# Expansion by source in halves of eight tiles, with 448-byte rows and a ScalarE copy

## The chip, the cores and the metric

The kernel runs on one core of a Trainium2 chip. The metric is the time of one execution in microseconds (us). A profile of one execution shows the engines PE (TensorE; PEld is its weight load), DVE (VectorE), ACT (ScalarE), POOL (GpSimd) and SP (SyncE, which here issues DMAs), and the DMA queues.

## The reference

Four graph layers run in a row on 12500 nodes of 64 features and 212500 edges, each layer behind a layer norm and a residual sum. The change touches the two middle ones:

```
# second layer: graph convolution
h   = features * deg_out ** -0.5 @ weight
rst = segment_sum(h[src], dst) * deg_in ** -0.5 + bias
# third layer: messages with edge features
msg = relu(x[src] + edge_attr)
agg = segment_sum(msg, dst)
h   = relu((x + agg) @ W1 + b1) @ W2 + b2
```

What matters here is `h[src]` and `x[src]`: one row of 64 numbers for every edge, read from the node table by the edge's source.

## The kernel before

The edges are sorted by source and padded to 1760 tiles of 128. `split_parts` writes the node table in SBUF as three bfloat16 parts (`m.parts`: high, middle and low, `PARTS` = 192 columns), whose sum is the fp32 value. `expand_by_source` (L1459) then makes one row per edge by a matmul with a one-hot matrix, writes the rows to DRAM, and `sum_by_target` (second layer) or `sum_messages_by_target` (third) fetches them in the order of the targets and sums them. The words "stage two" and "stage three" below mean the runs of `expand_by_source` for layer 2 and layer 3.

A stage works through 110 chunks of 16 tiles (`SB` = 16, 2048 edges); ten chunks are one body of a loop. No scheduler orders the work: each engine has its own hand-written list, and semaphores join them.

- **SP** (`step`, L1512): for chunk n it waits until the one-hot matrix of n is made, loads the lanes of chunk n+5 (L1496, 2048 bf16 numbers to all 128 partitions, 512 KB), in stage three also the edge features of chunk n+5 (L1500, 512 KB), and then stores the rows of chunk n (L1510) when they are ready.
- **DVE**: `turn` (L1555) makes the one-hot matrix of the next chunk from the lanes. In stage two `reach` (L1563, six instructions) prepares six small matmuls that locate groups, `put` (L1576) copies half of the results from PSUM to the rows as bf16, and `take` (L1568) reads the located groups. In stage three `add` (L1586, L1588, L1590) sums three parts and the edge features.
- **PE** (L1621 to L1651): for each quarter `u` of a chunk (four tiles, two PSUM banks) four matmuls of 192 columns (L1639). The columns' place in `m.parts` comes from the sorted block numbers: `run_values` (L1628, helper L801) loads eight numbers from SBUF into registers, twice a chunk. In stage two the odd quarters are followed by three small matmuls (L1647).
- **ACT**: in stage two it copies the even quarters (L1669); in stage three it applies Relu (L1666).
- **POOL**: in stage two it writes the target number of each edge into the last word of its row (L1686).

A row of stage two is 98 words (`ROW2`), 392 bytes: 192 bf16 parts, a one, and the target. `sum_by_target` gathers four rows (1568 bytes) per partition with an indirect DMA of POOL (L1936), reads the target number on DVE (L1832), and sums on PE. Beside that it splits edge features, which SP loads (L1767) and DVE prepares (L1805 to L1814).

Of the kernel before, what the change touches and what calls it, by code (L numbers as in the profile page):

```python
# [49 lines left out]
ROW2 = PARTS // 2 + 2  # L50
# [74 lines left out]
def allocate(nc, ctx):  # L125
# [41 lines left out]
    at += SB * P  # L167
    m.row_out = arena[:, at:at + 5 * SB * ROW2].rearrange("p (c t f) -> p c t f", c=5, f=ROW2)
# [16 lines left out]
    attr_onehot = arena[:, at:at + CB * P // 2]  # L185
    assert at + CB * P // 2 <= ARENA
# [40 lines left out]
    m.onehot_attr = [part.bitcast(BF16).rearrange("p (f s) -> p f s", s=CB) for part in (attr_onehot, tables[:, free:free + CB * P // 2])]  # L227
# [1231 lines left out]
def expand_by_source(nc, m, layer):  # L1459
# [9 lines left out]
    with ExitStack() as ctx:  # L1469
        s = sems(nc, "blank", "turned", "expanded", "put_act", "put_dve", "dst", "summed", "added", "row", "reached", "found", "taken", "zeros")  # L1470
# [14 lines left out]
        def sum_of(u, n):  # L1485

            return quad[:, 2 * u:2 * u + 2, 0:2 * PARTS].rearrange("p k (t f) -> p k t f", f=PARTS)[:, :, :, n * D:(n + 1) * D]

        def rows_of(ring_, c, u):

            return ring_[:, c % 5, 4 * u:4 * u + 4, :].rearrange("p (k t) f -> p k t f", t=2)

        @block.sync
        def _(sp):
            def lanes(n, c):
                sp.dma_start(m.lane_rows[:, c % 5, :], m.lanes_dram[bass.ds(n * (SB * P), SB * P)].partition_broadcast(P)  # L1496
                             ).then_inc(lanes_in[c % 5], 16)

            def attr(n, c):
                sp.dma_start(m.attr_rows[:, c % 5, :, :], records[:, bass.ds(n * SB, SB), REC_ATTR:REC]).then_inc(attr_in[c % 5], 16)  # L1500

            def store(n, c):
                if layer == 2:
                    sp.wait_ge(s["put_act"], n * 2 + 2 + 2)
                    sp.wait_ge(s["put_dve"], n * 2 + 2 + 2)
                    sp.wait_ge(s["dst"], n + 1)
                else:
                    sp.wait_ge(s["row"], n * 4 + 4)
                settle(sp)
                sp.dma_start(to_dram[bass.ds(n * (SB * P), SB * P), :].rearrange("(t p) f -> p t f", p=P), out[:, c % 5, :, :]  # L1510
                             ).then_inc(stored[c % 5], 16)

            def step(n, c, more):
                if more:
                    sp.wait_ge(s["turned"], n + 1)
                    settle(sp)
                    lanes(n + 5, c)
                if more == "all":
                    if layer == 3:
                        sp.wait_ge(s["added"], n * 4 + 4 + 4)  # L1520
# [12 lines left out]
            for c in range(chunks):  # L1533
                step((BODIES - 1) * chunks + c, c, "all" if c < chunks - 5 else "lanes" if c == chunks - 5 else "")
            for c in range(5):
                sp.wait_ge(stored[c], 16 * (TS // SB // 5))
            sp.wait_ge(s["zeros"], 16)

        @block.vector
        def _(dve):  # L1540
            v = nc.vector
            if layer == 2:
                v.memset(out16[:, :, :, PARTS:PARTS + 2].rearrange("p c t f -> p (c t) f"), 1.0).then_inc(s["blank"], 1)
                dve.wait_ge(s["blank"], 1)
            v.sem_inc(s["expanded"], 2 * 4)
            v.sem_inc(s["put_dve"], 2)
            v.sem_inc(s["taken"], 2)
            v.sem_inc(s["added"], 4)

            def turn(i, c):  # L1550
                n = i * chunks + c
                dve.wait_ge(lanes_in[c % 5], i * (chunks // 5 * 16) + c // 5 * 16 + 16)

                dve.wait_ge(s["expanded"], n * 4 + 4)
                v.tensor_scalar(m.turned16[:, c % 2, :], m.lane_rows[:, c % 5, :], m.lane_no[:, :], None, ALU.is_equal  # L1555
                                ).then_inc(s["turned"], 1)

            def reach(i, c):
                n = i * chunks + c

                dve.wait_ge(s["expanded"], n * 4 + 4)
# [4 lines left out]
            def take(i, c, u):  # L1566
                n = i * chunks + c
                v.tensor_reduce(m.found[:, bass.ds(n * SET + u // 2 * (SET // 2), SET // 2)],  # L1568
                                quad[:, 2 * u + 1, FOUND:FOUND + 3 * (SET // 2)].rearrange("p (e n) -> p e n", n=3), AX, ALU.add
                                ).then_inc(s["taken"], 1)  # L1570

            def put(i, c, u):
                n = i * chunks + c
                dve.wait_ge(s["expanded"], n * 4 + u + 1 + 2 * 4)
                to = rows_of(out16, c, u)[:, :, :, 0:PARTS]
                v.tensor_copy(to, quad[:, 2 * u:2 * u + 2, 0:2 * PARTS].rearrange("p k (t f) -> p k t f", f=PARTS)).then_inc(s["put_dve"], 1)  # L1576
                take(i, c, u)

            def add(i, c, u):
                n = i * chunks + c  # L1580
                k = n * 4 + u
                dve.wait_ge(s["expanded"], k + 1 + 2 * 4)
                if u == 0:
                    dve.wait_ge(attr_in[c % 5], i * (chunks // 5 * 16) + c // 5 * 16 + 16)
                to, attr = rows_of(out, c, u), rows_of(m.attr_rows, c, u)
                v.tensor_tensor(to, sum_of(u, 0), attr, ALU.add).then_inc(s["summed"], 1)  # L1586
                dve.wait_ge(s["summed"], 2 * k + 1)
                v.tensor_tensor(to, to, sum_of(u, 1), ALU.add).then_inc(s["summed"], 1)  # L1588
                dve.wait_ge(s["summed"], 2 * k + 2)
                v.tensor_tensor(to, to, sum_of(u, 2), ALU.add).then_inc(s["added"], 1)  # L1590

            def body(i, first):
                for c in range(chunks):
# [6 lines left out]
                    if not first or c >= 5:  # L1600
# [18 lines left out]
        def _(pe):  # L1619
            parts = m.parts.rearrange("p b f -> p (b f)")  # L1620
            with pe.Fori(0, BODIES) as i:  # L1621
                for c in range(chunks):
                    n = i * chunks + c
                    pe.wait_ge(s["turned"], n + 1)
                    for u in range(4):
                        k = n * 4 + u
                        if u % 2 == 0:
                            numbers = run_values(nc, ENG.PE, m.sorted_block[:, bass.ds(n * SB + 4 * u, 8)], NB)  # L1628

                        if layer == 3:  # L1630
                            pe.wait_ge(s["added"], k + 1)
                        elif u % 2:
                            pe.wait_ge(s["put_dve"], n * 2 + u // 2 + 1)
                            pe.wait_ge(s["taken"], n * 2 + u // 2 + 1)
                        else:
                            pe.wait_ge(s["put_act"], n * 2 + u // 2 + 1)
                        settle(pe)
                        for j in range(4):
                            done = nc.tensor.matmul(quad[:, 2 * u + j // 2, j % 2 * PARTS:(j % 2 + 1) * PARTS],  # L1639
                                                    m.turned16[:, c % 2, (4 * u + j) * P:(4 * u + j + 1) * P],  # L1640
                                                    parts[:, bass.ds(numbers[4 * (u % 2) + j] * PARTS, PARTS)], start=True, stop=True)
                        if layer == 2 and u % 2:
                            for e in range(SET // 2):
                                g = u // 2 * (SET // 2) + e
                                if e == 0:
                                    pe.wait_ge(s["reached"], n * SET + g + SET // 2)
                                done = nc.tensor.matmul(quad[:, 2 * u + 1, FOUND + 3 * e:FOUND + 3 * e + 3],  # L1647
# [6 lines left out]
        def _(act):  # L1654
            a = nc.scalar

            def body(i, first):
                for c in range(chunks):
# [3 lines left out]
                    for u in range(4):  # L1662
                        if layer == 3:
                            act.wait_ge(s["added"], n * 4 + u + 1 + 4)
                            rows = out[:, c % 5, 4 * u:4 * u + 4, :]
                            a.activation(rows, rows, ACT.Relu).then_inc(s["row"], 1)  # L1666
                        elif u % 2 == 0:
                            act.wait_ge(s["expanded"], n * 4 + u + 1 + 2 * 4)
                            a.activation(rows_of(out16, c, u)[:, :, :, 0:PARTS],  # L1669
                                         quad[:, 2 * u:2 * u + 2, 0:2 * PARTS].rearrange("p k (t f) -> p k t f", f=PARTS),  # L1670
                                         ACT.Copy).then_inc(s["put_act"], 1)

            act.sem_inc(s["put_act"], 2)
# [4 lines left out]
        if layer == 2:  # L1678
            @block.gpsimd
            def _(pool):  # L1680
                def body(i, first):
                    for c in range(chunks):
# [3 lines left out]
                        nc.gpsimd.tensor_copy(m.row_out[:, c % 5, :, ROW2 - 1:ROW2],  # L1686
# [10 lines left out]
def sum_by_target(nc, m, a, layer):  # L1697
# [9 lines left out]
    with ExitStack() as ctx:  # L1707
# [72 lines left out]
        def _(dve):  # L1780
# [39 lines left out]
            with dve.Fori(0, BODIES_D) as i:  # L1820
                if layer == 2:
                    add_bias(i * SHARE)
                for c in range(BODY_D):
# [7 lines left out]
                    if layer == 2:  # L1831
                        v.tensor_tensor(lanes.rearrange("p (g t) -> p g t", t=GRAN),  # L1832
                                        m.ring2[:, c % deep, :, ROW2 - 1].rearrange("p (g t) -> p g t", t=GRAN),
# [1083 lines left out]
```

## Time and profile before

| | us |
|---|---|
| three runs | 8924.55, 8933.99, 8934.04 (median 8933.99) |
| profiled execution | 8922.76 |
| its span, first to last instruction | 8920.1 |
| stage two, first instruction to the first gather after it | 3132.9 to 3900.8 |
| summing of layer 2, first to last gather | 3900.8 to 4814.7 |
| stage three, first to last store issued | 4913.6 to 5588.3 |

Over the whole span PE is busy 71%, DVE 66%, POOL 55% and ACT 28%, but these are means over stages with different limits; the two expansions are 1440 us of the span and are read by themselves. Times in rows are microseconds from the start of the span. A row of a timeline gives the start, the duration, the engine, the line, the operation, its tiles and shape, how many (x), and in brackets how long the engine was idle before and what ended that. "issue" there means that the profile shows no semaphore or DMA for which the engine waited. PEq or PEldq marks instructions of PE's sequencer.

### The profile page before, as it was taken

To read this page: it belongs to the slowest core of one execution; us is meant where nothing else is said; L and a number is where in the kernel's file an instruction comes from. 1 tells how busy PE (TensorE), PEld (TensorE's weight loads), DVE (VectorE), ACT (ScalarE), POOL (GpSimd) and SP (SyncE) were. 2 spreads that over 40 slices of the span, in tenths; PEclk is the share of its full clock that TensorE was granted. 3 is DMA by queue.
4 is the path that set the end of the run, shared out by engine and by line. 5 is a ranking of instruction groups with operands and counts; after the bars stand their busy time and mean duration, and the time that the engine had idled before them with its cause. 6 is when DMAs were issued, how large, how long until landed. Compare 5 with 4: busy or idle time off the path is not lost. (4 is left out here: it accounts for less than half of the span.)

```text
span 8920.1 us, 183726 instructions
## 1 busy us (share of the span) xinstructions
PE 6289.7 (71%) x35446; PEld 4927.1 (55%) x35447; DVE 5909.6 (66%) x18166; ACT 2529.7 (28%) x8033; POOL 4865.1 (55%) x4975
## 2 busy tenths in 40 slices
PE   2688888888847645556664555788668888888886
PEld 1577777777735433345553222566456666666664
DVE  8566666666669755568887888899554444444444
ACT  5355555555511222211110222111112221222222
POOL 0477777777756200047773000677347777777773
PEclk9555555555555655568886555999855555555556
DMA  6655555454546399987786999666633333333333
GB/s 133 152 154 149 156 148 154 149 156 147 156 97 139 72 190 195 195 198 224 230 226 130 246 257 257 181 181 178 92 111 82 80 80 80 81 81 80 82 80 30
DMA packets 1822628, 1295.50 MB, mean 145 GB/s; under 512 B 1262870, under 2 KB 1643574, under 8 KB 1820576
## 3 DMA queue, kind: packets, MB, share of 16 engines
q1 hardware_dynamic: 1580112, 841.10, 39.9%
q0 software_dynamic: 200704, 415.20, 17.9%
q10 hardware_dynamic: 40912, 29.67, 1.5%
q14 instruction: 638, 5.23, 0.2%
q8 instruction: 262, 4.29, 0.2%
HBM read 923.76 MB, written 361.78 MB: 144 GB/s over the span
## 5 line engine op out<-in xcount | busy, mean ns | idle before, releaser
L1138 POOL DMA_INDIRECT sorted_edges<-arena,idx x1664 | 1619.0, 973 | 727.8 <-issue 638.7
L2253 POOL DMA_INDIRECT arena<-node_table,idx x1760 | 1660.4, 943 | 557.0 <-issue 388.9
L1053 PE MATMUL banks<-arena,edge_tables 128*128 x3520 | 1164.7, 439 | 288.3 <-DVE edge_tables L982 233.8
L2229 PE MATMUL banks<-arena 128*128 128x64 f32 x3520 | 1214.1, 448 | 0.0
L1639 PE MATMUL banks<-arena 128*128 x3520 | 670.9, 361 | 769.2 <-issue 435.2
L1053 PEld LDWEIGHTS banks<-arena,edge_tables 128*128 128x128 f32 x3520 | 898.5, 317 | 417.6 <-issue 393.3
L2224 PE MATMUL banks<-arena 128*64 128x65 f32 x3520 | 843.0, 343 | 401.0 <-ACT arena L2240 400.3
L2128 POOL DMA_INDIRECT arena<-expanded,idx x576 | 544.6, 945 | 1003.5 <-DVE idx L2005 788.5
L2229 PEld LDWEIGHTS banks<-arena 128*128 128x128 f32 x3520 | 883.4, 311 | 210.2
L2240 ACT ACTIVATE arena<-arena 128x64 f32<-128x64 f32 x1760 | 450.1, 257 | 1787.2 <-DVE arena L2192 1781.6
L2199 DVE TENSOR_TENSOR arena<-arena,banks 128x64 f32 x1760 | 387.8, 220 | 820.2 <-PE banks L2229 792.8
L1639 PEld LDWEIGHTS banks<-arena 128*128 128x128 bf16 x3520 | 367.0, 104 | 1012.2 <-issue 931.8
L955 DVE SCALAR_TENSOR_TENSOR edge_tables<-iota_row,edge_tables,banks 128x99 f32<-128x99 f32 x1664 | 528.9, 318 | 594.2 <-PE banks L1035 582.4
L2224 PEld LDWEIGHTS banks<-arena 128*64 128x64 f32 x3520 | 509.5, 206 | 627.4 <-ACT arena L2240 451.9
L1936 POOL DMA_INDIRECT arena<-expanded,idx x576 | 659.3, 1145 | 274.9 <-issue 146.5
L1104 ACT ACTIVATE arena<-arena,edge_tables 128x64 f32<-128x64 f32 x1664 | 446.2, 337 | 912.8 <-DVE arena L992 903.4
L982 DVE TENSOR_SCALAR edge_tables<-arena,shift_row 128x128 f32 x1760 | 526.6, 299 | 171.4 <-issue 94.1
L1085 ACT ACTIVATE edge_tables<-base,edge_tables 128x99 bf16<-128x99 bf16 x1664 | 491.0, 368 | 201.3 <-issue 132.2
L1033 PE MATMUL banks<-per_node,from 128*128 128x99 bf16 x1664 | 467.0, 281 | 72.2 <-DVE per_node L945 70.6
L1063 PE MATMUL banks<-w_pair,arena 128*128 128x128 f32 x1664 | 485.8, 448 | 0.0
L1039 PE MATMUL banks<-edge_tables,per_node 128*99 128x99 bf16 x1664 | 451.0, 271 | 47.9 <-ACT edge_tables L1085 47.9
L2192 DVE TENSOR_TENSOR arena<-arena,banks 128x64 f32<-128x64 f32 x1760 | 375.9, 215 | 162.6 <-DMA arena<-node_table,idx 157.4
(426 smaller groups left out, 11712.5 us busy)
## 6 DMA issues: line engine op xcount, KB each, us to landing
arena<-sorted_edges SPq DMA_DIRECT2D x220, 524.0 KB
arena<-lanes_dram SPq DMA_DIRECT2D x222, 512.0 KB, 8.0
expanded<-arena SPq DMA_DIRECT2D x110, 784.0 KB, 8.0
arena<-in_attr_rows SPq DMA_DIRECT2D x576, 130.0 KB
arena<-sorted_edges SPq DMA_DIRECT2D x110, 536.0 KB
arena<-row_keys SPq DMA_DIRECT2D x110, 512.0 KB
arena<-sorted_edges SPq DMA_DIRECT2D x110, 512.0 KB, 5.6
expanded<-arena SPq DMA_DIRECT2D x110, 512.0 KB
```

The source lines that it names most:

```text
L955: v.scalar_tensor_tensor(m.junk[:, j % 2, 0:BUCKETS], m.iota_row[:, 0:BUCKETS], m.bucket[:, bass.ds(n, 1)], rank, ALU.is_equal, ALU.mult, ...
L982: v.tensor_scalar(m.onehot[:, j % 4, :], m.row_ring[:, bass.ds(slots[j] * P, P)], first_lane[:, j:j + 1], None, ALU.is_equal).then_inc(s[" ...
L1053: nc.tensor.matmul(m.psum[j % 4][:, 0:D], m.onehot[:, j % 4, :], m.support[:, bass.ds(blocks[j] * D, D)], start=True, stop=True).then_inc( ...
L1063: product = nc.tensor.matmul(m.psum[bank_of(n)][:, e * P:(e + 1) * P], m.pair_ring[c % 2][:, pair * P:(pair + 1) * P], m.w_pair[:, :], sta ...
L1085: a_.activation(m.below[:, (QUAD * n + e) % 8, 0:BUCKETS], m.base16[:, 0:BUCKETS], ACT.Sign, bias=m.pack[:, bass.ds(t, 1), 1], scale=-SHRU ...
L1138: nc.gpsimd.indirect_dma_start(m.sorted, bass.IndirectOffsetOnAxis(ap=m.idx[:, j % (4 * CH):j % (4 * CH) + 1], axis=0), m.out_ring[:, slot ...
L1639: done = nc.tensor.matmul(quad[:, 2 * u + j // 2, j % 2 * PARTS:(j % 2 + 1) * PARTS], m.turned16[:, c % 2, (4 * u + j) * P:(4 * u + j + 1) ...
L1936: nc.gpsimd.indirect_dma_start(to, None, rows, bass.IndirectOffsetOnAxis(ap=m.idx[:, c % aims * groups + g:c % aims * groups + g + 1], axis=0)
L2128: nc.gpsimd.indirect_dma_start(m.ring3[:, at:at + GRAN * row], None, rows, bass.IndirectOffsetOnAxis(ap=m.idx[:, c % aims * groups + g:c % ...
L2224: nc.tensor.matmul(m.psum[GRAM][0:D, 0:RW], row[:, 0:D], row, start=False, stop=False, skip_group_check=True)
L2229: nc.tensor.matmul(m.psum[j % 4][:, 0:D], m.onehot8[:, c % 4, j % CB, :], row[:, 0:D], start=True, stop=True).then_inc(s["summed"], 1)
L2253: nc.gpsimd.indirect_dma_start(slots[:, j % SLOTS, 0:D], None, m.table, bass.IndirectOffsetOnAxis(ap=m.idx[:, j % SLOTS:j % SLOTS + 1], ax ...
```

## The change

Both expansions are now written for halves `h` of eight tiles (four PSUM banks each) in place of quarters of four.

- PE loads the 16 block numbers of a chunk with one `run_values` at the top of the chunk, ahead of the wait for the one-hot matrix. It waits per half, not per quarter. In stage two both halves are followed by their three small matmuls, as the odd quarters were.
- In stage two ACT copies each whole half (1536 numbers per partition) in one instruction, after DVE's `take` of that half. DVE copies nothing. The semaphores `put_act` and `put_dve` become one, `put`.
- In stage three DVE's three sums and ACT's Relu run on 512 numbers per partition in place of 256, half as often.
- Rows of stage two are 112 words, 448 bytes. The target number keeps its place (word 97); words 98 to 111 are set to zero once, by a second memset, for which ACT waits before it first frees the PSUM halves. The store carries 896 KB per chunk (784 KB before), a gather 1792 bytes per partition (1568).
- One one-hot buffer of `sum_by_target` moves from the arena to the edge tables to make room.

```diff
-ROW2 = PARTS // 2 + 2
+ROW2 = 112
+COUNT2 = PARTS // 2
+DST2 = COUNT2 + 1
...
     def store(n, c):
         if layer == 2:
-            sp.wait_ge(s["put_act"], n * 2 + 2 + 2)
-            sp.wait_ge(s["put_dve"], n * 2 + 2 + 2)
+            sp.wait_ge(s["put"], n * 2 + 2 + 2)
             sp.wait_ge(s["dst"], n + 1)
         else:
-            sp.wait_ge(s["row"], n * 4 + 4)
+            sp.wait_ge(s["row"], n * 2 + 2)
...
 def body(i, first):   # DVE
     for c in range(chunks):
         turn(i, c + 1)
         if layer == 2:
             reach(i, c)
-        for u in range(4):
+        for h in range(2):
             if layer == 3:
-                add(i, c, u)
-            elif u % 2:
-                put(i, c, u)
+                add(i, c, h)
+            else:
+                take(i, c, h)
...
 # PE
+numbers = run_values(nc, ENG.PE, m.sorted_block[:, bass.ds(n * SB, SB)], NB)
 pe.wait_ge(s["turned"], n + 1)
-for u in range(4):
-    if u % 2 == 0:
-        numbers = run_values(nc, ENG.PE, m.sorted_block[:, bass.ds(n * SB + 4 * u, 8)], NB)
+for h in range(2):
...
 # ACT
-            elif u % 2 == 0:
-                act.wait_ge(s["expanded"], n * 4 + u + 1 + 2 * 4)
+            else:
+                act.wait_ge(s["expanded"], n * 2 + h + 1 + 2 * 2)
+                act.wait_ge(s["taken"], n * 2 + h + 1 + 2)
```

In the two listings below the names in brackets are semaphores as the built program calls them: lane_26 is `turned`, ended_27 `expanded`, rows_28 is `put_act` before and `put` after, variance_35 is `taken`; kept_39 and brought_40 belong to the loads of lanes. ISA rows set registers or wait.

On PE, between the two halves of a chunk of stage two, the order before is:

```order
L1647 MATMUL banks<-edge_tables,arena 128x3
L801 ISA
L801 TENSOR_LOAD target_plan
L1636 REGISTER_ALU
L1639 ISA [waits rows_28]
L1639 MATMUL banks<-arena 128x192
```

and after:

```order
L1638 MATMUL banks<-edge_tables,arena 128x3
L1625 REGISTER_ALU
L1630 ISA [waits rows_28,variance_35]
L1630 MATMUL banks<-arena 128x192
L1630 ISA
```

The register load is gone from this place; the other one, at the top of the chunk, stays and loads 16 numbers.

On DVE, one chunk of stage two before:

```order
L1555 TENSOR_SCALAR arena<-arena,lane_no 128x2048 [waits ended_27,brought_40]
L1563 TENSOR_SCALAR arena<-iota_row,edge_tables 99x128 [waits ended_27]
L1563 TENSOR_SCALAR arena<-iota_row,edge_tables 99x128 x5
L1576 CAST arena<-banks 128x4x192 [waits ended_27]
L1568 TENSOR_REDUCE edge_tables<-banks 128x3
```

and after:

```order
L1557 TENSOR_SCALAR arena<-arena,lane_no 128x2048 [waits ended_27,kept_39]
L1565 TENSOR_SCALAR arena<-iota_row,edge_tables 99x128 [waits ended_27]
L1565 TENSOR_SCALAR arena<-iota_row,edge_tables 99x128 x5
L1571 TENSOR_REDUCE edge_tables<-banks 128x3 [waits ended_27] x2
L1557 TENSOR_SCALAR arena<-arena,lane_no 128x2048 [waits ended_27,brought_40]
```

The pair of CAST and TENSOR_REDUCE stood twice in a chunk; both copies have left DVE, and the two reductions now wait for PE themselves.

## Rows read from the trace of the kernel before

**Rows 1.** Windows: length, busy PE, PEld, DVE, ACT, POOL, clock, DMA share, GB/s.

```profile
3500.00:3700.00 200.00, 106.22 (x645) 67.10 (x644) 114.57 (x324) 47.30 (x59) 7.77 (x30) 0.50 1.13 196
...
5200.00:5400.00 200.00, 104.12 (x526) 54.58 (x524) 177.69 (x424) 54.53 (x131) 0.00 (x0) 0.50 1.12 256
```

**Rows 2.** One tile (expanded rows): durations in ns min/median/max, first and last start.

```profile
L1936 POOL DMA_INDIRECT arena<-expanded,idx x576: 940/977/2739, 3900.8 to 4814.7; - x192
...
L1525 SPq DMA_DIRECT2D expanded<-zero x2: 332/336/339, 3132.9 to 4913.6; - x2
```

**Rows 3.** Timeline of one chunk of stage two.

```profile
3505.37 0.74 DVE L1555 TENSOR_SCALAR arena<-arena,lane_no 128x2048 bf16<-128x2048 bf16 x1
...
3505.40 1.46 PE L1639 MATMUL banks<-arena 128*128 x8 [1.01 <-issue]
3505.60 0.40 SPq L1510 DMA_DIRECT2D expanded<-arena  x1
...
3506.03 1.26 DVE L1563 TENSOR_SCALAR arena<-iota_row,edge_tables 99x128 bf16<-99x128 f32 x6
...
3506.25 0.81 ACT L1669 ACTIVATE arena<-banks 128x768 bf16<-128x768 f32 x1 [1.92 <-PE banks L1639]
...
3506.87 0.48 PE L1647 MATMUL banks<-edge_tables,arena 99*128 x3
...
3507.39 0.96 DVE L1576 CAST arena<-banks 128x768 bf16<-128x768 f32 x1
...
3509.48 1.46 PE L1639 MATMUL banks<-arena 128*128 x8 [2.13 <-issue]
...
3512.23 0.34 PE L1639 MATMUL banks<-arena 128*128 x1 [1.04 <-issue]
```

**Rows 4.** Register loads: two of stage two; four-number loads of 3950 to 4780.

```profile
L801 PEldq TENSOR_LOAD <-target_plan x1: 591/591/591, 3504.4 to 3504.4; - x1
...
L801 PEldq TENSOR_LOAD <-target_plan x1: 1786/1786/1786, 3507.3 to 3507.3; - x1
...
L801 PEldq TENSOR_LOAD <-target_plan x130: 330/334/622, 3952.6 to 4777.5; - x130
```

**Rows 5.** Waits of SP, 3200 to 3800: total us, times, longest.

```profile
SPq L796 <- DVE arena L1576: 316.6, 88, 4.3
```

**Rows 6.** ACT copies of 512 and 256 numbers just ahead of stage two.

```profile
L1440 ACT ACTIVATE arena<-banks x4: 395/583/598, 3127.1 to 3128.6; 128x512 bf16<-128x512 f32 x3, 128x256 bf16<-128x256 f32 x1
```

**Rows 7.** DMA: a store's issue, packets of 3880-3881.75, 3882-3883.5, then 5586-5591.5.

```profile
3879.04 0.38 SPq L1510 DMA_DIRECT2D expanded<-arena  x1
...
q1 hardware_dynamic: 1167, 0.46, 96.4%
...
q1 hardware_dynamic: 725, 0.28, 115.6%
...
q1 hardware_dynamic: 4631, 1.18, 95.9%
```

**Rows 8.** Stage three: SP's timeline, then DVE's wait and adds, 4960 to 5540.

```profile
5251.72 2.07 SPq L1496 DMA_DIRECT2D arena<-lanes_dram  x1
5254.14 0.39 SPq L1500 DMA_DIRECT2D arena<-sorted_edges  x1
5254.84 2.59 SPq L1510 DMA_DIRECT2D expanded<-arena  x1
5257.74 2.06 SPq L1496 DMA_DIRECT2D arena<-lanes_dram  x1
...
DVE arena L1555 <- DMA arena<-lanes_dram: 32.8, 78, 0.8
...
L1590 DVE TENSOR_TENSOR arena<-arena,banks 128x256 f32<-128x256 f32 x382 | 160.6, 420 | 13.1
```

**Rows 9.** Summing of layer 2: gather queue of 4000-4600, a wait of 3950-4780.

```profile
q0 software_dynamic: 24539, 76.95, 45.8%
...
DVE edge_tables L1805 <- DMA arena<-in_attr_rows: 104.3, 110, 4.7
```

More of the change, by code:

```diff
@@ L167, in allocate @@
     at += SB * P
+    assert ROW2 * 5 * SB <= 10 * SB * D and DST2 < ROW2
     m.row_out = arena[:, at:at + 5 * SB * ROW2].rearrange("p (c t f) -> p c t f", c=5, f=ROW2)
@@ L184, in allocate @@
     at += SB * P
-    attr_onehot = arena[:, at:at + CB * P // 2]
-    assert at + CB * P // 2 <= ARENA
+    assert at <= ARENA
     at = NB * PARTS
@@ L226, in allocate @@
     assert AIMED * 3 <= TD
-    m.onehot_attr = [part.bitcast(BF16).rearrange("p (f s) -> p f s", s=CB) for part in (attr_onehot, tables[:, free:free + CB * P // 2])]
+    m.onehot_attr = [part.bitcast(BF16).rearrange("p (f s) -> p f s", s=CB) for part in (tables[:, 4 * TP:4 * TP + CB * P // 2], tables[:, free:free + CB * P // 2])]
     m.attr_parts = [tables[:, TSX + n * PARTS:TSX + (n + 1) * PARTS] for n in range(2)]
@@ L1469, in expand_by_source @@
     with ExitStack() as ctx:
-        s = sems(nc, "blank", "turned", "expanded", "put_act", "put_dve", "dst", "summed", "added", "row", "reached", "found", "taken", "zeros")
+        s = sems(nc, "blank", "turned", "expanded", "put", "dst", "summed", "added", "row", "reached", "found", "taken", "zeros")
         lanes_in = ring(nc, "lanes_in", 5)
@@ L1483, in expand_by_source, with sum_of, half_of @@
         FOUND = 2 * PARTS
[L1485 to L1491, printed above, removed]
+        HALF = SB // 2
+        def sum_of(h, n):
+            return quad[:, 4 * h:4 * h + 4, 0:2 * PARTS].rearrange("p k (t f) -> p k t f", f=PARTS)[:, :, :, n * D:(n + 1) * D]
+        def half_of(ring_, c, h):
+            return ring_[:, c % 5, HALF * h:HALF * h + HALF, :].rearrange("p (k t) f -> p k t f", t=2)
         @block.sync
@@ L1519, in step @@
                     if layer == 3:
-                        sp.wait_ge(s["added"], n * 4 + 4 + 4)
+                        sp.wait_ge(s["added"], n * 2 + 2 + 2)
                         settle(sp)
@@ L1543, in _ @@
                 v.memset(out16[:, :, :, PARTS:PARTS + 2].rearrange("p c t f -> p (c t) f"), 1.0).then_inc(s["blank"], 1)
-                dve.wait_ge(s["blank"], 1)
-            v.sem_inc(s["expanded"], 2 * 4)
-            v.sem_inc(s["put_dve"], 2)
+                v.memset(out16[:, :, :, PARTS + 4:2 * ROW2].rearrange("p c t f -> p (c t) f"), 0.0).then_inc(s["blank"], 1)
+            v.sem_inc(s["expanded"], 2 * 2)
             v.sem_inc(s["taken"], 2)
-            v.sem_inc(s["added"], 4)
+            v.sem_inc(s["added"], 2)
             def turn(i, c):
@@ L1552, in turn @@
                 dve.wait_ge(lanes_in[c % 5], i * (chunks // 5 * 16) + c // 5 * 16 + 16)
-                dve.wait_ge(s["expanded"], n * 4 + 4)
+                dve.wait_ge(s["expanded"], n * 2 + 2)
                 v.tensor_scalar(m.turned16[:, c % 2, :], m.lane_rows[:, c % 5, :], m.lane_no[:, :], None, ALU.is_equal
@@ L1559, in reach @@
                 n = i * chunks + c
-                dve.wait_ge(s["expanded"], n * 4 + 4)
+                dve.wait_ge(s["expanded"], n * 2 + 2)
                 for e in range(SET):
@@ L1564, in reach, with take, add @@
                                     None, ALU.is_ge).then_inc(s["reached"], 1)
-            def take(i, c, u):
+            def take(i, c, h):
                 n = i * chunks + c
-                v.tensor_reduce(m.found[:, bass.ds(n * SET + u // 2 * (SET // 2), SET // 2)],
-                                quad[:, 2 * u + 1, FOUND:FOUND + 3 * (SET // 2)].rearrange("p (e n) -> p e n", n=3), AX, ALU.add
+                dve.wait_ge(s["expanded"], n * 2 + h + 1 + 2 * 2)
+                v.tensor_reduce(m.found[:, bass.ds(n * SET + h * (SET // 2), SET // 2)],
+                                quad[:, 4 * h + 3, FOUND:FOUND + 3 * (SET // 2)].rearrange("p (e n) -> p e n", n=3), AX, ALU.add
                                 ).then_inc(s["taken"], 1)
[L1572 to L1583, printed above, removed]
+            def add(i, c, h):
+                k = (i * chunks + c) * 2 + h
+                dve.wait_ge(s["expanded"], k + 1 + 2 * 2)
+                if h == 0:
                     dve.wait_ge(attr_in[c % 5], i * (chunks // 5 * 16) + c // 5 * 16 + 16)
-                to, attr = rows_of(out, c, u), rows_of(m.attr_rows, c, u)
-                v.tensor_tensor(to, sum_of(u, 0), attr, ALU.add).then_inc(s["summed"], 1)
+                to, attr = half_of(out, c, h), half_of(m.attr_rows, c, h)
+                v.tensor_tensor(to, sum_of(h, 0), attr, ALU.add).then_inc(s["summed"], 1)
                 dve.wait_ge(s["summed"], 2 * k + 1)
-                v.tensor_tensor(to, to, sum_of(u, 1), ALU.add).then_inc(s["summed"], 1)
+                v.tensor_tensor(to, to, sum_of(h, 1), ALU.add).then_inc(s["summed"], 1)
                 dve.wait_ge(s["summed"], 2 * k + 2)
-                v.tensor_tensor(to, to, sum_of(u, 2), ALU.add).then_inc(s["added"], 1)
+                v.tensor_tensor(to, to, sum_of(h, 2), ALU.add).then_inc(s["added"], 1)
             def body(i, first):
@@ L1599, in body @@
                         reach(i, c)
-                    if not first or c >= 5:
+                    if layer == 3 and (not first or c >= 5):
                         dve.wait_ge(stored[c % 5], i * (chunks // 5 * 16) + c // 5 * 16)
-                    for u in range(4):
+                    for h in range(2):
                         if layer == 3:
-                            add(i, c, u)
-                        elif u % 2:
-                            put(i, c, u)
+                            add(i, c, h)
+                        else:
+                            take(i, c, h)
             body(0, True)
@@ L1623, in _ @@
                     n = i * chunks + c
+                    numbers = run_values(nc, ENG.PE, m.sorted_block[:, bass.ds(n * SB, SB)], NB)
                     pe.wait_ge(s["turned"], n + 1)
-                    for u in range(4):
-                        k = n * 4 + u
-                        if u % 2 == 0:
-                            numbers = run_values(nc, ENG.PE, m.sorted_block[:, bass.ds(n * SB + 4 * u, 8)], NB)
+                    for h in range(2):
                         if layer == 3:
[L1631 to L1634, printed above, removed]
-                        else:
-                            pe.wait_ge(s["put_act"], n * 2 + u // 2 + 1)
+                            pe.wait_ge(s["added"], n * 2 + h + 1)
+                        else:
+                            pe.wait_ge(s["put"], n * 2 + h + 1)
+                            pe.wait_ge(s["taken"], n * 2 + h + 1)
@@ L1637, in _ @@
                         settle(pe)
[L1638 to L1642, printed above, removed]
+                        for j in range(HALF):
+                            t = HALF * h + j
+                            done = nc.tensor.matmul(quad[:, t // 2, t % 2 * PARTS:(t % 2 + 1) * PARTS],
+                                                    m.turned16[:, c % 2, t * P:(t + 1) * P],
+                                                    parts[:, bass.ds(numbers[t] * PARTS, PARTS)], start=True, stop=True)
@@ L1643, in _ @@
+                        if layer == 2:
                             for e in range(SET // 2):
-                                g = u // 2 * (SET // 2) + e
+                                g = h * (SET // 2) + e
                                 if e == 0:
                                     pe.wait_ge(s["reached"], n * SET + g + SET // 2)
-                                done = nc.tensor.matmul(quad[:, 2 * u + 1, FOUND + 3 * e:FOUND + 3 * e + 3],
+                                done = nc.tensor.matmul(quad[:, 4 * h + 3, FOUND + 3 * e:FOUND + 3 * e + 3],
@@ L1661, in body @@
                         act.wait_ge(stored[c % 5], i * (chunks // 5 * 16) + c // 5 * 16)
-                    for u in range(4):
+                    for h in range(2):
                         if layer == 3:
-                            act.wait_ge(s["added"], n * 4 + u + 1 + 4)
-                            rows = out[:, c % 5, 4 * u:4 * u + 4, :]
+                            act.wait_ge(s["added"], n * 2 + h + 1 + 2)
+                            rows = out[:, c % 5, HALF * h:HALF * h + HALF, :]
                             a.activation(rows, rows, ACT.Relu).then_inc(s["row"], 1)
-                        elif u % 2 == 0:
-                            act.wait_ge(s["expanded"], n * 4 + u + 1 + 2 * 4)
[L1669 to L1673, printed above, removed]
+                        else:
+                            act.wait_ge(s["expanded"], n * 2 + h + 1 + 2 * 2)
+                            act.wait_ge(s["taken"], n * 2 + h + 1 + 2)
+                            a.activation(half_of(out16, c, h)[:, :, :, 0:PARTS],
+                                         quad[:, 4 * h:4 * h + 4, 0:2 * PARTS].rearrange("p k (t f) -> p k t f", f=PARTS),
+                                         ACT.Copy).then_inc(s["put"], 1)
+            if layer == 2:
+                act.wait_ge(s["blank"], 2)
+                act.sem_inc(s["put"], 2)
             body(0, True)
@@ L1685, in body @@
                         settle(pool)
-                        nc.gpsimd.tensor_copy(m.row_out[:, c % 5, :, ROW2 - 1:ROW2],
+                        nc.gpsimd.tensor_copy(m.row_out[:, c % 5, :, DST2:DST2 + 1],
                                               m.dst_sorted[:, bass.ds((i * chunks + c) * SB, SB)].unsqueeze(2)).then_inc(s["dst"], 1)
@@ L1832, in _ @@
                         v.tensor_tensor(lanes.rearrange("p (g t) -> p g t", t=GRAN),
-                                        m.ring2[:, c % deep, :, ROW2 - 1].rearrange("p (g t) -> p g t", t=GRAN),
+                                        m.ring2[:, c % deep, :, DST2].rearrange("p (g t) -> p g t", t=GRAN),
                                         m.block_at[:, bass.ds(n * groups, groups)].unsqueeze(2).to_broadcast([P, groups, GRAN]),
```

## Prediction

> **What bounds the kernel now.** The change lies in two stages of 110 chunks and, by the longer rows, in the summing after the first of them, so I read the windows by stage first, then the timeline of one chunk, then the DMA queues.
>
> Stage two runs from 3132.9 to 3900.8, 768 us [rows 2]. DVE issues 11 instructions a chunk there (one turn, six for reach, two copies, two reductions), and 324 of them in 200 us [rows 1] are 29.45 chunks: 6.79 us a chunk. PE is busy 53% of that, DVE 57%, and the DMA share stands above 1 at 196 GB/s [rows 1]; so both PE and the queues could be the limit. The timeline decides. PE's first block starts at 3505.40, its small matmuls end at 3507.35, then PE is idle for 2.13 us "on issue"; the second block runs from 3509.48 to 3511.19 (the next start at 3512.23 less 1.04), and 1.04 us are idle again [rows 3]. That closes the period of 6.83: blocks of 1.95 and 1.71, gaps of 2.13 and 1.04. Both gaps hold a register load, of 1.786 and 0.591 us [rows 4]; the rest of each gap, 0.34 and 0.45, is waits and address arithmetic. Nothing else is late there: the copies of the bank halves end (3507.06 on ACT) well before PE comes back to them. SP waits for DVE 316.6 us in 600 [rows 5], so the stores wait for compute and not the other way round. Stage two is bound by PE's own list, half of whose idle time is one slow register load.
>
> Why that load takes three times as long as the other isn't in the rows; what they show is where it stands. It starts 1.7 us after a store was issued at 3505.60 [rows 3, 4], while the store's rows leave SBUF: the store issued at 3879.04 has 1892 of its 2048 packets between 3880 and 3883.5 [rows 7], so a store occupies the queues until about 4.5 us after its issue. The fast load comes 5.6 us after the previous store's issue, one period back.
>
> Stage three is another case. SP issues lanes, features and store one behind the other, 2.07, 0.39 and 2.59 us with 0.3 us between them, and begins again after 6.02 us [rows 8]: there is no room in its list for a wait on compute. DVE, 89% busy [rows 1], waits for lanes in 78 chunks of about 96 [rows 8], though these are ordered five chunks ahead. Stage three is bound by SP and the queue behind it, at 256 GB/s [rows 1].
>
> **The change part by part.** Stage two, on PE. One register load goes, the other loads 16 numbers. Four numbers take 0.334 us and eight 0.591 [rows 4], 64 ns each, so 16 come to 1.11 us (at least 0.59, if the load has a flat part; at most 2.3, if it is slowed as the slow one is). With 0.45 us of waits around it, two blocks of 1.71 (the 0.24 us that the first block lost to reach goes: DVE's turn and reach now begin behind a reduction, 0.16, and three of the six reach steps are done 1.5 us after the previous chunk, while PE needs them at 2.7) and 0.25 us between the halves, for which the bounds are 0 and 0.45, PE's period is 1.11 + 0.45 + 1.71 + 0.25 + 1.71 = 5.23 us.
>
> On ACT a copy of 1536 numbers replaces one of 768. 256 take 0.395, 512 about 0.59 [rows 6] and 768 take 0.81 [rows 3], so 1536 come to 1.47 us, two of them to 2.9 us a chunk. The copy of a half starts 0.25 us after PE is done (take is now ahead of it) and ends 1.7 us after; PE wants the same banks back after 1.11 + 0.45 + 1.71 + 0.25 = 3.5 us. So the new wait costs nothing with 1.8 us to spare; what is queued behind it on ACT is only the next copy, and the store on SP, which goes out about 0.9 us later than now, with five row buffers behind it. DVE loses two copies of 0.96 us [rows 3] a chunk, worth nothing, because DVE isn't the limit.
>
> Stage two, on the queues. A chunk moves 896 KB of rows and 512 KB of lanes, 1.442 MB. Rows of 256 bytes take 18.2 ns a packet and hold that for 5.5 us; rows of 392 bytes take 23.1 ns at first and 38.3 ns in the later part of the same store (share times 16 engines times the window, over the packets) [rows 7]. For 448 bytes the line through 256 and 392 gives 25 ns; with today's slow part it would be 33 to 42. The nearest row for the sum of rows and lanes is stage three, with 256-byte rows and the same lanes: at its 256 GB/s a chunk takes 5.63 us. At today's 196 GB/s it takes 7.36 us. I take the first, because 448 bytes, like 256 and unlike 392, is a whole number of 64-byte pieces and the slow part appears with 392 alone; that this is the reason is a guess.
>
> Against this stands the Trainium skill: "DMA: Bandwidth & Descriptors", section Specifications, says that transfers under 512 B make the DMA read, modify and write. By that rule 448 bytes would be as badly off as 392, and the sum would go by 196 GB/s. The 256-byte stores don't show such a loss.
>
> So the queues (5.63) and PE (5.23, and more when a store slows the load) lie close, and I take 5.65 us a chunk: (6.79 - 5.65) x 110 = 125 us gained. The ends: 5.23, or 172 us, and 7.36, or 63 us lost.
>
> Stage three: six of twelve DVE sums go. From 256 (0.42) [rows 8] to 768 numbers (0.96) [rows 3] DVE needs about 1.05 ns a number, so a sum of 512 takes 0.69 in place of 0.84 and DVE gains 0.9 us a chunk. SP's list is as long as before, so I book 0; what DVE gains it waits longer for lanes.
>
> Summing of layer 2: gathers grow by 14%. Their queue takes 45.8% of the 16 engines in 600 us [rows 9], so about 6.5% more, 59 us over 915 us if nothing hid it. DVE is the busiest engine there and waits 104.3 us of 830 for edge features behind those gathers [rows 9]; if that wait grows by a tenth, the loss is 12 us. Bounds 0 and 59; I take 12. The larger memset at the start hides behind the loading of the first lanes.
>
> Sum against the profiled execution: 8922.8 - 125 + 12 = 8810 us. The median of the runs is 11 us above that execution and the fastest run 2 us; I put the median at 8815.
>
> **The rivals.**
> - *The store slows the long load in every chunk.* The store is issued about 1.9 us after the last matmul of its chunk, and with a period of 5.2 the load starts 3.3 us behind it, within the 4.5 us. With the 1.2 us that the slow load loses now, the period is 6.43 and the gain 40 us: 8900. Against it: at 6.4 us the next load starts behind the store and is fast again.
> - *The rows stay slow, and the queues take over: slower.* If they move no more than 196 GB/s, the chunk takes 7.36 us, 63 us are lost and 12 more in the summing: 9000. It decides as soon as the rate stays below 1.442 MB in 6.79 us, 212 GB/s. For it speak the DMA share above 1 already now and the page's rule; against it the fast 256-byte rows and that SP waits for DVE now.
> - *The queues give way entirely.* Then PE's 5.23 stands: 8922.8 - 172 + 12, or 8768 for the median.
> - *Stage three gains too*, because SP's long issues follow DVE after all: 99 us more, 8716. Its SP rows speak against it.
> - *Little happens*, since the rate settles near 212 GB/s and one limit takes the place of the other: 8930.
>
> **How the numbers follow.** Forecast 8815: 0.47. Load slowed: 0.15. PE alone: 0.15. Slower: 0.10. Little: 0.07. Stage three too: 0.06. A measurement of this kernel tells 0.2%, 18 us, from no change. Faster by more than that: 0.47 + 0.15 + 0.15 + 0.06 = 0.83; within: 0.07; slower: 0.10. The range reaches from just under PE's case to just over the slowed load, 8750 to 8905, and leaves out stage three, the slower case and half of little.
>
> **What would show it.** In stage two: one register load a chunk on PE, of 1.1 us or up to 2.3 beside a store; a period of 5.2 to 5.8; ACT copies of 1.47 us; the queue at 250 GB/s or more and 448-byte packets near 25 ns. In stage three: SP without waits, the same 6.0 us, and DVE waiting longer for lanes. In the summing: the wait of L1805 somewhat over 104 us. I am wrong if the 448-byte rows are slower than 30 ns on the mean, if SP stops waiting for compute in stage two, or if the period of stage three moves.

## The result, and the profile after

The changed kernel takes 8782.95 us (median of 4 runs, 8779.7 to 8794.44) where the kernel before, on the same chip, takes 8932.7: a ratio of 0.9837, interval 0.9819 to 0.9854. The profiled execution of after is its slowest, 8794.44 us with a span of 8792.7; against the span before (8920.1), 127.4 us are gone. The medians lie 149.8 apart, because the profiled execution of before is faster than all its timed runs. Where the 127.4 went, read from the first and last starts of the rows of the expanded tile (columns as in [rows 2]):

```profile
L1930 POOL DMA_INDIRECT arena<-expanded,idx x576: 943/977/2746, 3738.7 to 4673.7; - x192
...
L1528 SPq DMA_DIRECT2D expanded<-zero x2: 332/338/343, 3135.4 to 4777.1; - x2
```

Stage two runs from 3135.4 to 3738.7, 603.3 us where it took 767.9 [rows 2]: -164.6. The summing of layer 2 follows, from the first gather to the last one ahead of stage three: 935.0 where the kernel before takes 913.9, +21.1. Stage three, from its store of zeros to the first gather of layer 3 (5460.0, before 5600.0), takes 683.0 against 686.4. What is left, 19.5 us later in sum, is spread over the gaps, the summing of layer 3 and the work before and behind, none of it over 9 us. So the gain has one place, stage two, and the summing gives an eighth of it back. The windows of both stages (columns as in [rows 1]):

```profile
3300.00:3500.00 200.00, 121.19 (x825) 96.66 (x825) 85.38 (x340) 108.58 (x75) 8.75 (x38) 0.54 0.96 270
5060.00:5260.00 200.00, 94.86 (x525) 62.26 (x522) 153.24 (x229) 40.95 (x65) 0.00 (x0) 0.53 1.12 257
```

In stage two the queues' share fell from 1.13 to 0.96 while they move 270 GB/s in place of 196 [rows 1]; DVE's 340 instructions, nine a chunk, make 37.8 chunks in 200 us, 5.3 us each (5.31 over 80 chunks). In stage three the queues' share and rate stayed (1.12, 257 GB/s), and only the engines have less to do (DVE 153 us of 200, before 178). One chunk of stage two, from the timeline:

```profile
3392.16 1.46 PE L1630 MATMUL banks<-arena 128*128 x8 [1.93 <-ACT arena L1661]
...
3393.41 0.38 PE L1638 MATMUL banks<-edge_tables,arena 99*128 x3
...
3393.93 1.46 PE L1630 MATMUL banks<-arena 128*128 x8
3394.13 1.45 ACT L1661 ACTIVATE arena<-banks 128x1536 bf16<-128x1536 f32 x1 [2.11 <-DVE edge_tables L1571]
3395.18 0.34 PE L1638 MATMUL banks<-edge_tables,arena 99*128 x3
...
3395.87 1.45 ACT L1661 ACTIVATE arena<-banks 128x1536 bf16<-128x1536 f32 x1 [0.29 <-DVE edge_tables L1571]
3397.41 1.46 PE L1630 MATMUL banks<-arena 128*128 x8 [1.88 <-ACT arena L1661]
```

Blocks of 1.63 and 1.59 us, 0.14 between them, then a gap of 1.89. The trace puts that gap down to ACT, whose copy ends at 3397.32. The code says otherwise: PE's first half waits for the copy of the first half of the chunk ahead, which ended at 3395.58. What fills the gap is PE's one register load, of 1.43 us at 3395.5. Below are that load, all loads in 500 us of the stage (min/median/max in ns), what SP waits for (us, times, longest) and the queue's packets, MB and share:

```profile
L803 PEldq TENSOR_LOAD <-target_plan x1: 1432/1432/1432, 3395.5 to 3395.5; - x1
...
L803 PEldq TENSOR_LOAD <-target_plan x95: 1108/1464/1797, 3198.8 to 3698.1; - x95
```

```profile
SPq L798 <- ACT arena L1661: 216.6, 95, 3.0
```

```profile
q1 hardware_dynamic: 207648, 135.74, 97.1%
```

The 448-byte packets take 27.3 ns on the mean (all packets in the trace between the stores of chunks 20 and 100), the 392-byte ones before 38.8. Then the two waits that the prediction priced, DVE for lanes in stage three (4830 to 5400) and DVE for features in the summing (3790 to 4640), and the gather queue of 3840 to 4440; before they were 32.8, 104.3 and 45.8% [rows 8, 9]:

```profile
DVE arena L1557 <- DMA arena<-lanes_dram: 116.9, 93, 1.6
```

```profile
DVE edge_tables L1799 <- DMA arena<-in_attr_rows: 126.8, 118, 5.0
```

```profile
q0 software_dynamic: 24134, 86.54, 49.6%
```

### The profile page after: what moved, and what is told of

It is laid out like the page before. It is cut to its first block and busy times, and to the rows that moved or that the text cites. A ratio compares the mean times of both kernels' runs of the same rounds, so it can differ in the third digit from the quotient of the medians.

```text
span 8792.7 us, 180824 instructions
## 1 busy us (share of the span) xinstructions
PE 6229.7 (71%) x35446; PEld 4996.4 (57%) x35447; DVE 5657.6 (64%) x17287; ACT 2626.5 (30%) x7813; POOL 4871.1 (55%) x4975
## 5 line engine op out<-in xcount | busy, mean ns | idle before, releaser
L1630 PE MATMUL banks<-arena 128*128 x3520 | 637.2, 359 | 675.7 <-DVE arena L1585 337.3
L1630 PEld LDWEIGHTS banks<-arena 128*128 128x128 bf16 x3520 | 418.6, 119 | 832.9 <-issue 773.3
L1887 PE MATMUL banks<-arena,edge_tables 128*128 128x192 bf16 x2304 | 319.6, 290 | 252.9 <-DVE arena L1808 251.4
```

The costliest lines, as they stand in the source:

```text
L1630: done = nc.tensor.matmul(quad[:, t // 2, t % 2 * PARTS:(t % 2 + 1) * PARTS], m.turned16[:, c % 2, t * P:(t + 1) * P], parts[:, bass.ds(nu ...
```

## The experiments

Theory: PE's second register load and the slow 392-byte rows each held stage two near 6.8 us a chunk. Rivals: the load alone, the rows alone, or the halves and ACT's copies. Ratios are to the kernel before on the same chip (8956.5 to 8958.1 us there). The last three columns are taken between the stores of chunks 20 and 100.

| kernel | ratio, interval | stage two us | us a chunk | GB/s | row's packet, mean ns |
|---|---|---|---|---|---|
| e1_row98 | 1.0006, 0.9996 to 1.0016 | 771.5 | 6.84 | 194 | 41.7 |
| e2_wide_rows | 1.002, 1.001 to 1.0029 | 764.1 | 6.77 | 213 | 26.2 |
| e4_one_load_wide | 0.983, 0.9814 to 0.9846 | 590.8 | 5.19 | 277 | 28.2 |
| e5_two_loads | 0.9916, 0.9899 to 0.9932 | 666.2 | 5.88 | 245 | 26.2 |
| e7_changed_again | 0.9839, 0.9826 to 0.9853 | 602.0 | 5.30 | 272 | 27.9 |
| e8_quarters_again | 0.9835, 0.9822 to 0.9848 | 590.9 | 5.20 | 277 | 28.3 |
| e9_row104 | 0.9828, 0.981 to 0.9846 | 603.0 | 5.30 | 259 | 27.2 |
| e10_shifted | 0.9841, 0.9824 to 0.9859 | 605.9 | 5.34 | 270 | 30.0 |
| e11_row110 | 1.0067, 1.0051 to 1.0084 | 799.4 | 7.10 | 200 | 46.0 |
| e12_row100 | 0.9875, 0.9858 to 0.9891 | 644.6 | 5.73 | 234 | 36.4 |
| e13_shift2 | 1.018, 1.0163 to 1.0197 | 911.1 | 8.13 | 177 | 55.3 |
| e14_quarters_row104 | 0.9827, 0.9811 to 0.9844 | 590.3 | 5.19 | 265 | 27.8 |

**e1_row98: the changed kernel with the old rows.**

```diff
-ROW2 = 112
+ROW2 = PARTS // 2 + 2
```

> The changed kernel with rows of 98 words (392 bytes) as before; all else (halves, one register load, ACT's copy) as changed. It separates the row's width from the rest. Theory (PE's list sets the period, and the narrow rows keep the queues too slow for it): a chunk moves 1.296 MB, at 196 to 212 GB/s 6.1 to 6.6 us; stage two 680 to 740 us against 768 before and 603 in the changed kernel; summing of layer 2 back at about 914 (935 in the changed kernel); 20 to 80 us faster than before. Rival (the width is without effect on stage two, PE alone sets it): period 5.3, stage two 600 to 610, summing 914, about 165 us faster than before and some 20 faster than the changed kernel.

The whole gain is gone, further than the theory put it: 6.84 us a chunk, as before. Part of the distance is a slip of the expectation: 784 and 512 KB are 1.327 MB in the unit of the prediction, not 1.296, and at 196 GB/s they take 6.77 us. Here the queue sets the end. SP waits for no compute any more; its own lanes issue takes 5.4 to 6.5 us in three chunks of the timeline where it took about 2, and DVE waits for lanes (one such issue, then the waits of 3200 to 3700):

```profile
3405.00 6.48 SPq L1500 DMA_DIRECT2D arena<-lanes_dram  x1
```

```profile
DVE arena L1556 <- DMA arena<-lanes_dram: 203.8, 73, 3.9
```

**e2_wide_rows: the kernel before with 448-byte rows, nothing else.**

```diff
-ROW2 = PARTS // 2 + 2
+ROW2 = 112
+DST2 = PARTS // 2 + 1
```

> The kernel before with rows of 448 bytes alone: quarters, two register loads of eight, and copies shared by ACT and DVE stay. Theory (PE's two loads set the period, the rows only matter once those are gone): period 6.6 to 6.8, stage two 750 to 770, summing 20 us longer, 0 to 20 us slower than before. Rival (the rows are the gain, the register loads were slow because the narrow store was): period below 6.3, stage two below 715, 30 us or more faster than before.

No gain either, but for the other reason. Its window (columns as in [rows 1]) has the same work per time as before while the queues' share falls from 1.13 to 0.74, and PE's gaps of 2.05 and 1.01 us stand nearly as they were (window, then timeline):

```profile
3300.00:3500.00 200.00, 107.01 (x649) 67.64 (x649) 113.76 (x322) 47.83 (x59) 6.30 (x30) 0.50 0.74 214
```

```profile
3402.80 1.46 PE L1640 MATMUL banks<-arena 128*128 x8 [2.05 <-issue]
...
3405.53 1.46 PE L1640 MATMUL banks<-arena 128*128 x8 [1.01 <-issue]
```

**e4_one_load_wide: the kernel before with 448-byte rows and one load; quarters and shared copies stay.**

```diff
+                    numbers = run_values(nc, ENG.PE, m.sorted_block[:, bass.ds(n * SB, SB)], NB)
...
-                        if u % 2 == 0:
-                            numbers = run_values(nc, ENG.PE, m.sorted_block[:, bass.ds(n * SB + 4 * u, 8)], NB)
```

> The kernel before with rows of 448 bytes and one register load of 16 numbers a chunk; quarters and the copies shared by ACT and DVE stay. Theory (one load less and the wide rows are the whole gain): period 5.3 to 5.5, stage two 600 to 630, the same total as the changed kernel within 25 us. Rival (halves and the copy by ACT alone are needed, because DVE's copies stand ahead of turn and reach): period 5.8 or more, stage two 660 or more, 55 us or more slower than the changed kernel.

These two edits give the whole gain. The load is at its bare length here, and the queue moves more than in the changed kernel (window, then load):

```profile
3300.00:3500.00 200.00, 133.53 (x853) 88.33 (x850) 150.07 (x425) 62.45 (x78) 10.59 (x38) 0.53 1.03 278
```

```profile
L801 PEldq TENSOR_LOAD <-target_plan x96: 1102/1105/1261, 3204.4 to 3698.2; - x96
```

**e5_two_loads: the changed kernel with a load of eight numbers ahead of each half.**

```diff
-                    numbers = run_values(nc, ENG.PE, m.sorted_block[:, bass.ds(n * SB, SB)], NB)
...
+                        numbers = run_values(nc, ENG.PE, m.sorted_block[:, bass.ds(n * SB + HALF * h, HALF)], NB)
```

> The changed kernel with two register loads of eight numbers, one ahead of each half; all else as changed. Theory (the second load is what the period lost): 0.6 us more if neither is slowed by a store, 1.3 more if one is; period 5.7 to 6.6, stage two 650 to 740, 45 to 135 us slower than the changed kernel. Rival (loads hide behind waits that take their place): period 5.3 to 5.5, within 25 us of the changed kernel.

The second load costs 0.57 us a chunk (5.88 against 5.30 in e7), 64 us of stage two. Nine in ten of its loads take 0.59 to 1.21 us, not the 1.79 of the slow one before: at another place in the chunk the same load has another length. Beside e2, which has the same rows and two loads too but works in quarters, e5 shows something else: 5.88 us a chunk against 6.77. So while two loads stand, halves and ACT's copies are worth about 0.9 us a chunk; half of that is shorter gaps on PE (1.10 and 1.52 us in a chunk of e5), the rest shorter blocks.

**e7_changed_again and e8_quarters_again: the changed kernel and e4's on one chip.**

> The changed kernel again, on the chip of the next run, so that the two can be compared. All theories: stage two about 603 us (period 5.3), summing 935, ratio to before about 0.984.

> Again the kernel before with rows of 448 bytes and one register load a chunk, quarters, copies shared by ACT and DVE. Theory (halves and the copy by ACT alone bring nothing; they only move the register load into the store's time, where it takes 1.47 us in place of 1.11): stage two 590 to 595 us, 5 to 15 us faster than the changed kernel. Rival (the copy by ACT alone is worth something that the other chip hid): slower than the changed kernel by 5 us or more.

The totals can't be told apart; the 5 to 15 us that e8 was to be faster are not there. Quarters are 11 us shorter in stage two (590.9 against 602.0) and lose as much in stage three and the summing of layer 3 (696.6 + 775.1 against 694.7 + 766.6). Why the summing of layer 3 differs is open: e2, in quarters too, has 763.5 there. With one load, halves and ACT's copies bring nothing to the time.

**e9_row104 and e10_shifted: 416-byte rows; 448-byte rows stored 32 bytes further on in DRAM** (the values read by the later layers are changed by it).

```diff
-ROW2 = 112
+ROW2 = 104
```

```diff
+    SHIFT = 8
...
+    m.expanded2_shifted = whole[SHIFT:SHIFT + rows_count * ROW2].rearrange("(r f) -> r f", f=ROW2)
...
-        to_dram = m.expanded2 if layer == 2 else m.expanded3
+        to_dram = m.expanded2_shifted if layer == 2 else m.expanded3
```

> The changed kernel with rows of 104 words: 416 bytes, 13 times 32 but 6.5 times 64. It tells why rows of 392 bytes are slow. Theory 64 (a row must be whole pieces of 64 bytes): packets 36 ns or more, stage two at the queue's limit of 195 to 215 GB/s, period 6.4 to 7.0, about 100 to 150 us slower than the changed kernel. Rival 32 (whole pieces of 32 bytes are enough): packets 25 to 28 ns, period 5.3, and the summing 5 to 10 us shorter than with 448 bytes. Rival size (no piece matters, longer rows are just better): packets about 32 ns, period 5.6 to 6.2.

> The changed kernel, but stage two stores every row 32 bytes further on in DRAM, so that each row of 448 bytes begins and ends within a piece of 64 bytes; the gathers read from the old places, so the values that the later layers use are other numbers. Size and count of all transfers are as in the changed kernel. Theory 64: packets 36 ns or more, period above 6.3. Rivals 32 and size: packets 27 ns, period 5.3.

Both are as fast as the changed kernel, so whole 64-byte pieces, the guess of the prediction, are not the reason. Another point is settled: with 4.5% fewer bytes in a chunk (e9) the period is the same 5.30 us, and e4 and e8 move the same bytes as the changed kernel in 5.19 and 5.20, so in the changed kernel the queue is not the limit.

**e11_row110, e12_row100, e13_shift2: rows of 440 and 400 bytes; 448-byte rows stored 8 bytes further on** (as e10 with `SHIFT = 2`; later values changed).

```diff
-ROW2 = 112
+ROW2 = 110
```

```diff
-ROW2 = 112
+ROW2 = 100
```

> The changed kernel with layer-2 rows of 440 bytes (27.5 pieces of 16 bytes, 13.75 pieces of 32), larger than the 416 and 448 bytes that went at 27 to 28 ns a packet. Theory 'pieces' (a row must be a whole number of 16- or 32-byte pieces): packets 38 ns or more, period of a chunk 6.8 us or more since each row is longer than 392 bytes, stage two 750 to 800 us, time 8940 to 8990 us on the chip where the changed kernel takes 8812. Rival 'size' (a row over some length between 392 and 416 bytes is cheap, whatever its divisors): packets 27 to 29 ns, period 5.3 us, stage two 600 us, time 8800 to 8815 us.

> The changed kernel with layer-2 rows of 400 bytes: 25 pieces of 16 bytes, 12.5 pieces of 32. If pieces of 32 bytes decide: packets 38 to 42 ns, period 6.8 us, stage two 770 us, time 8955 us as with 392 bytes. If pieces of 16 bytes decide: packets 26 to 28 ns, period 5.3 us, stage two 600 us, time 8800 us. The rival 'size' allows either.

> The changed kernel with its 448-byte rows stored 8 bytes further on in DRAM (the values that the later layers read are changed by it, the amount of work is not). If it is the place of a row in DRAM that costs (both its ends off a piece's edge): packets 38 ns or more, period over 6.5 us, stage two over 730 us, time over 8930 us. If it is the row's length alone, or its place in SBUF: packets 27 to 30 ns, period 5.3 us, stage two 600 to 606 us, time 8810 us as with the shift by 32 bytes.

Size as the reason falls: 440 bytes are slower than 416, and the 9018 us of e11 lie above even the 8940 to 8990 foretold for pieces. The length in itself falls too: the same 448 bytes, 8 bytes further on, double the packet's time (queue rows of 3200 to 3700, in the order e11, e12, e13):

```profile
q1 hardware_dynamic: 155115, 100.34, 116.1%
```

```profile
q1 hardware_dynamic: 192398, 117.13, 117.4%
```

```profile
q1 hardware_dynamic: 135349, 88.55, 117.9%
```

What orders them is how many boundaries between neighbouring rows fall inside a 32-byte piece (if the tensor begins on a piece's edge): none with 416, 448 and the shift by 32 (27 to 30 ns), half with 400 (36), three quarters with 392 and 440 (39 to 42, and 46), all with the shift by 8 (55). Pieces of 16 would have made 400 bytes fast. e12 fell between its two forecasts, and the count of boundaries was made after it, so the order fits the runs but was not foretold. Nor can e12's period be put down to the queue alone: DVE does not wait for lanes there (204 us of 500 in e1, 211 in e11, 250 in e13), and its register load, 1.83 us on the median against 1.46, makes up 0.37 of the 0.43 us that it loses to e7. The median packet is 24 to 26 ns in all of them; what grows is the tail, the slowest hundredth taking over 45 ns in the changed kernel, 187 ns before and 378 ns in e13 (packets of 3300 to 3600). That two writers of one piece hold each other up would fit, but is argued only: no run stored rows that end off an edge with no neighbour in the same piece.

**e14_quarters_row104: e4's two edits with 416-byte rows.**

```diff
+ROW2 = 104
+DST2 = PARTS // 2 + 1
```

> The kernel before with two edits alone: one register load of sixteen numbers per chunk, and rows of 416 bytes (quarters and the copies shared by VectorE and ScalarE stay). If it combines what the runs showed best: stage two 591 us as with 448-byte rows in quarters, summing of layer 2 931 us as with 416 bytes in halves, so some 9 us less than with 448-byte rows in quarters: 8795 to 8805 us on a chip where the changed kernel takes 8812. If the sums trade off (what one stage gains the next one gives back): 8805 to 8815.

Its total, 8802.5, lies where the two gains were to add up, but its rows show that they trade off: stage two 590.3, but summing of layer 2 936.7, not 931. It does not beat the changed kernel by more than a measurement tells; it reaches its time with two small edits.

## Why the prediction was right, and where not

- **Bound by PE's list: right, but half of it.** e2 shows that PE's list alone holds 6.77 us. That SP waited for DVE [rows 5] was read as room on the queues; e1 shows that, with PE relieved, they stop at 6.84. (SP's 216.6 us of waiting after prove as little by themselves; there e4 and e9 are the proof.) Two limits lay within about 1% of each other, and the prediction priced the second only as a rival that "takes over".
- **One load in place of two.** Priced at 1.11 us with 0.59 and 2.3 as bounds: 1.105 in e4, 1.46 in the changed kernel. The case "slowed in every chunk" held for 0.36 us of its 1.2. PE's period without slowing was put at 5.23; e4 has 5.19, the changed kernel 5.31, its blocks a little shorter than the 1.71 booked. What the second load costs hangs on the rest of the list: 1.58 us a chunk in quarters (e2 to e4), 0.57 in halves (e5 to e7).
- **The queue at 256 GB/s: the mis-sized term.** It set the forecast's 5.65 us. The queue moved 270, in e4 277, and e4 and e9 show that it wasn't the limit at all. So the mechanism was that of the rival "PE alone" (8768), with a partly slowed load. Worth 40 us of stage two: -164.6 against -125. For the profiled execution that is most of the account: 40 us less than the forecast's 8810 in stage two and 3 in stage three, 9 more in the summing, and 19.5 that nothing was booked for, together 8795 (measured 8794.4). The median came out 32 us under 8815; half of that is chance, because it lies 11 us below the profiled execution where 5 above were booked.
- **448-byte rows near 25 ns, not 33 to 42: right** (27.3), by a wrong reason, and in that lucky: whole pieces of 64 bytes were a guess, and e9 and e10 are fast without them. The Trainium skill ("DMA: Bandwidth & Descriptors", Specifications) says that under 512 B the DMA reads, modifies and writes. These runs don't show that limit: rows of 256, 416 and 448 bytes, all under 512, go without the loss that rows of 392, 400 and 440 have. No run gave stage two rows of 512 bytes or more, so what the rule itself costs is not shown.
- **ACT's longer copies and its later store at nothing: right** for the total once the load is one (e7, e8); the copies took 1.45 us for the 1.47 booked.
- **Stage three at 0: right.** SP's chain is as long as before, and DVE's gain, 0.9 us a chunk as booked and about 0.76 by the windows (177.7 us in 424 instructions, 153.2 in 229, 13 and 7 a chunk), turned into waiting for lanes, 116.9 us in place of 32.8.
- **Summing of layer 2 at 12 (0 to 59): 21.** The gather queue's share grew by 3.8 points, to 49.6%, a little more than half of the 14% by bytes (6.4 points); DVE's wait grew by 22 us, a fifth, where a tenth was booked.

## What to carry to other kernels

An engine that waits does not show that the resource behind it has room: before pricing a relief, work out at what period the next limit stands, and expect nothing from either edit alone where both stand at the same one. Lay rows that are written densely next to each other out so that each begins and ends on a whole 32 bytes, padding if need be: here packets 14% longer took 30% less time. Join register loads into one where they stand on the bounding engine's list, and look at where in the chunk the load falls, since its length depends on it.

## What was not expected of the hardware

Padding beats packing by 32-byte pieces, as above: 8 bytes of shift cost 309 us of stage two (911.1 against 602.0).

A register load's length varies threefold: eight numbers 0.59 or 1.79 us [rows 4], sixteen 1.11 in e4, 1.46 in the changed kernel, about 2.5 in stage three beside the stores. The prediction put it down to stores leaving SBUF. That fits the loads before: fast and slow ones both run beside DVE's copy, but the slow ones with 19 store packets in flight on the mean, the fast ones with 4. It doesn't fit e12: its load takes 1.83 us on the median (below) with 8 store packets in flight, about as many as in e4 (7) and in e13 (9), where it takes 1.11 and 1.13. What stands beside it in e12 alone of these three is DVE's reach, and the whole of its turn. DVE's turn by itself does little: in e5, four in five of the loads under 0.61 us run partly beside it. So both the stores and DVE's work may lengthen a load; no run changed one of them alone, and the cause stays open. The loads of e12, then of e13:

```profile
L803 PEldq TENSOR_LOAD <-target_plan x88: 1110/1831/2625, 3203.9 to 3696.5; - x88
```

```profile
L808 PEldq TENSOR_LOAD <-target_plan x62: 1107/1134/1277, 3202.7 to 3699.9; - x62
```
